# Eighteen expert gate products moved into the recurrence of the second layer, and kept in dead SBUF slots

## The reference

```python
# Mamba block: d_inner = 256, d_state = 16
def step(state, inp):
    dt_t, u_t, b_t, c_t, g_t = inp
    a = a_base[None] * (0.5 + g_t)[..., None]
    decay = jnp.exp(dt_t[..., None] * a)
    state = decay * state + dt_t[..., None] * b_t[:, None, :] * u_t[..., None]
    y_t = jnp.sum(state * c_t[:, None, :], axis=-1) + D_param * u_t
    return (state, y_t)
...
# experts: x is the normalised output of the Mamba block
#   y = sum over e of weight[e] * ((silu(x @ w_gate[e].T) * (x @ w_up[e].T)) @ w_down[e].T)
#   the shared expert (e = 16) has weight 1
```

## Time and profile before

| | |
|---|---|
| three runs | 650.7, 651.13, 652.67 us (median 651.13) |
| the profiled execution's own time | 651.55 us |
| its span, first to last instruction | 649.8 us |
| mean granted TensorE clock | 0.941 of full speed |
| busy: PE, DVE, ACT, POOL | 558.8, 529.8, 361.4, 393.9 us |

### The profile page before, as it was taken

One profiled execution on the slowest core, in us unless ns is written; L12 is line 12 of the kernel. 1 busy time (PEld: TensorE's weight loads), 2 busy tenths in 40 slices (PEclk: granted clock), 3 DMA queues, 4 the chain that ended last, 5 costly groups with the idle time before them and its releaser, 6 DMA issues.

```text
span 649.8 us, 6609 instructions
## 1 busy us (share of the span) xinstructions
PE 558.8 (86%) x1832; PEld 311.2 (48%) x1832; DVE 529.8 (82%) x729; ACT 361.4 (56%) x606; POOL 393.9 (61%) x345
## 2 busy tenths in 40 slices
PE   6698668899999978897868778878979999999997
PEld 3233222376768523333323223223345778888885
DVE  1979997656879678899999999999999857666674
ACT  4675323688123498767746535644455475555553
POOL 0035986752000202399999999999877546666664
PEclk9798977999799998899989868999989999999999
DMA  8000000800120002222223333331214334335330
GB/s 308 15 1 2 0 1 1 344 1 1 66 66 0 2 0 71 75 73 78 73 56 100 95 92 92 115 105 66 96 68 168 96 117 124 127 106 146 112 100 17
DMA packets 23796, 51.59 MB, mean 79 GB/s; under 512 B 2896, under 2 KB 3184, under 8 KB 23248
## 3 DMA queue, kind: packets, MB, share of 16 engines
q1 hardware_dynamic: 23760, 51.17, 24.2%
HBM read 49.83 MB, written 1.33 MB: 79 GB/s over the span
## 4 chain that ended last, share of the span: by engine, by line
PE 36%; DVE 22%; POOL 19%; issue 13%; ACT 9%; DMA 1%; POOLq 0%; DVEq 0%; SPq 0%; ACTq 0%
POOL h_parts L2163 9%; POOL arena L2028 8%; DVE arena L1948 7%; PE ps L1110 7%; PE ps L1045 6%; DVE arena L1923 4%; PE ps L716 3%; DVE arena L1676 3%; PE ps L895 2%; DVE ps L1660 2%; PE ps L912 1%; PE ps L830 1%; PE ps L833 1%; PE ps L831 1%; PE ps L1057 1%
## 5 line engine op out<-in xcount | busy, mean ns | idle before, releaser
L2028 POOL TENSOR_TENSOR arena<-arena 128x512 f32<-128x512 f32 x184 | 225.6, 1249 | 22.6 <-DVE arena L1948 18.5
L1045 PE MATMUL ps<-arena,core 128*128 128x512 f32 x256 | 137.4, 652 | 24.5 <-POOL arena L2028 23.1
L1948 DVE TENSOR_TENSOR_SCAN arena<-ps,carry,arena 128x512 f32<-128x512 f32 x128 | 158.2, 1291 | 0.0
L1505 ACT ACTIVATE ps<-arena,abase 128x512 f32<-128x512 f32 x128 | 88.3, 691 | 93.8 <-DVE arena L1948 92.2
L2163 POOL TENSOR_TENSOR h_parts<-arena,h_parts 128x512 fp32r<-128x512 f32 x68 | 87.7, 1290 | 60.9 <-ACT h_parts L1543 60.0
L1110 PE MATMUL ps<-x_parts,w_hi 128*128 128x512 f32 x272 | 100.7, 409 | 1.0 <-DVE arena L1948 0.5
L1045 PEld LDWEIGHTS ps<-arena,core 128*128 128x128 f32 x256 | 48.3, 201 | 87.2 <-POOL arena L2028 60.8
L1923 DVE TENSOR_TENSOR arena<-ps,arena 128x1024 f32<-128x1024 f32 x64 | 78.4, 1225 | 4.1 <-PE ps L1145 4.0
L2016 DVE TENSOR_TENSOR ps<-ps,arena 128x512 f32<-128x512 f32 x64 | 44.7, 698 | 41.8 <-PE ps L1110 32.9
L1551 ACT ACTIVATE arena<-ps 128x512 f32<-128x512 f32 x68 | 40.5, 597 | 60.5 <-PE ps L1110 60.4
L1110 PEld LDWEIGHTS ps<-x_parts,w_hi 128*128 128x128 f32 x272 | 51.4, 189 | 16.5 <-issue 2.0
(11 more groups left out here) (257 smaller groups left out, 959.3 us busy)
## 6 DMA issues: line engine op xcount, KB each, us to landing
arena<-c_rows SPq DMA_DIRECT2D x64, 256.0 KB, 3.1
arena<-weight_rows SPq DMA_DIRECT2D x64, 256.0 KB, 3.3
arena<-in_wB SPq DMA_DIRECT2D x2, 2048.0 KB, 12.3
arena<-in_wD SPq DMA_DIRECT2D x8, 384.0 KB, 4.1
arena<-in_cstB SPq DMA_DIRECT2D x1, 1368.0 KB, 5.6
wC<-in_wC SPq DMA_DIRECT2D x1, 1056.0 KB, 12.4
x<-in_x SPq DMA_DIRECT2D x4, 256.0 KB, 4.6
arena<-slot_rows SPq DMA_DIRECT2D x4, 256.0 KB, 3.8
```

Of the source, the lines that this page charges most:

```text
L1045: mm(bank(c + 2 * (i % 2)), CORE_("eye"), PRC[:, (2 * q + c) % PR_RING, :], start=False, stop=(n == NS - 1)).then_inc(*done(f"y{n}_{c}", i))
L1505: A(bank(6 + c), ch(DTG[:, c, :], i), ACT.Exp, scale=ABASE[:, c * NS + n:c * NS + n + 1]).then_inc(*done(f"dec{n}_{c}", i))
L1948: nc.vector.tensor_tensor_scan(ST[:, k % ST_RING, :], bank(6 + c), DBU[:, (2 * q + c) % DBU_RING, :], CARRY[:, k:k + 1], ALU.mult, ALU.add ...
L2028: mul = lambda o, a, b: nc.gpsimd.tensor_tensor(o, a, b, ALU.mult)
```

## The change

In words:

- The first 18 gate products (chunk 0 with all 17 experts, and chunk 1 with expert 0) are made by PE during the recurrence, one at the end of each of 18 turns between 31 and 60 (`EARLY_AT`), into PSUM bank 5. ACT copies each to an SBUF slot (`gate_copy`, at the end of the same turn), and the next one waits for that copy. In the expert phase their silu is taken in place from that slot.
- Bank 5 is kept free for them: from turn 30 on `b` has bank 4 alone, so `b(q)` waits for `dbu(q - 1)`, where it waited for `dbu(q - 2)`.
- To find slots, the ring DBU shrinks from 6 to 4 halves. `dbu(q)` thus waits for `st(q - 2)`, where it waited for `st(q - 3)`. The ring ROW shrinks from 8 to 7 rows.
- The down product lies four turns behind (LAG_E = 4), with five slots for its input where there were four.
- At the start of the expert phase `hu0` stands ahead of `y(60)` and `y(61)`, where `hg0` and `hg1` stood around them.

```diff
-LAG_E = 3
-W_SLOTS = 8
+LAG_E = 4
+H_PARTS = LAG_E + 1
+W_SLOTS = 7
...
-C_RING, DBU_RING, PR_RING, ST_RING = 4, 6, 2 * LAG, 8
+C_RING, DBU_RING, PR_RING, ST_RING = 4, 4, 2 * LAG, 8
...
+EARLY_AT = {31: 0, 32: 1, 33: 2, 34: 3, 35: 4, 36: 5, 37: 6, 38: 7, 40: 8, 41: 9, 42: 10, 45: 11, 47: 12, 49: 13, 51: 14, 52: 15, 54: 16, 60: 17}
+EARLY = len(EARLY_AT)
+ONE_BANK = 30
+def b_bank(q):
+    return 4 + q % 2 if q < ONE_BANK else 4
+def b_before(q):
+    return next((p for p in range(q - 1, -1, -1) if b_bank(p) == b_bank(q)), None)
...
             def gate_product(m):
                 i, e = divmod(m, E1 + 1)
                 pe.wait_ge(*upto("x_lo", i))
-                if i == 0:
-                    pe.wait_ge(*upto("w_lo", part_of(3 * e + 2)))
-                if m < 2:
-                    pe.wait_ge(*turn("dbu{}", NQ - 2 + m))
+                if m < EARLY:
+                    pe.wait_ge(*upto("w_lo", part_of(3 * e)))
+                if m < EARLY:
+                    pe.wait_ge(*(expert("hg_copy{}", m - 1) if m else turn("dbu{}", ONE_BANK - 1)))
+                elif m < EARLY + 2:
+                    pe.wait_ge(*(expert("hg_copy{}", EARLY - 1) if m % 2 else turn("dbu{}", NQ - 1)))
                 else:
                     pe.wait_ge(*expert("silu{}", m - 2))
-                product(bank(4 + m % 2), 3 * e, ...
+                product(bank(4 + m % 2 if m >= EARLY else 5), 3 * e, ...
...
                 if q >= 2:
-                    pe.wait_ge(*turn("dbu{}", q - 2))
-                mm(bank(4 + q % 2), sel[:, n, :], ...
+                    pe.wait_ge(*turn("dbu{}", b_before(q)))
+                mm(bank(b_bank(q)), sel[:, n, :], ...
...
                 side_work(q)
+                if q in EARLY_AT:
+                    gate_product(EARLY_AT[q])
             side_work(NQ)
-            gate_product(0)
+            up_product(0)
             y_sum(NQ - LAG)
-            gate_product(1)
             y_sum(NQ - LAG + 1)
-            up_product(0)
...
+            def gate_copy(m):
+                i, e = divmod(m, E1 + 1)
+                act.wait_ge(*upto(f"hg{e}", i))
+                if m in GAM_SLOT:
+                    act.wait_ge(*upto("x_mamba", GAM_SLOT[m]))
+                A(GATED[m], bank(5), ACT.Copy).then_inc(*done(f"hg_copy{e}", i))
             for q in range(NQ):
                 decays(q)
                 side_work(q)
+                if q in EARLY_AT:
+                    gate_copy(EARLY_AT[q])
...
-                act.wait_ge(*upto(f"hg{e}", i))
-                if q >= 2:
-                    act.wait_ge(*expert("hh{}", q - 2))
-                A(SG[:, q % 2, :], bank(4 + q % 2), ACT.Silu).then_inc(*done(f"silu{e}", i))
+                if q < EARLY:
+                    act.wait_ge(*upto(f"hg_copy{e}", i))
+                    A(GATED[q], GATED[q], ACT.Silu).then_inc(*done(f"silu{e}", i))
+                else:
...
```

More of the change, by code:

```diff
@@ L311, in sequences @@
             if 0 < m < TURNS:
-                pe += ([(f"hg{e}", mi)] if m > 1 else []) + [(f"hu{e}", mi)]
+                pe += ([(f"hg{e}", mi)] if m >= EARLY else []) + [(f"hu{e}", mi)]
         if m == 0:
-            pe += [("hg0", 0)] + y_names(q) + [("hg1", 0)] + y_names(q + 1) + [("hu0", 0)]
+            pe += [("hu0", 0)] + y_names(q) + y_names(q + 1)
         elif LAG <= q < NQ + LAG - 1:
@@ L329, in sequences @@
             pool.append(("w_lo", SPLIT_AT[q]))
+        if q in EARLY_AT:
+            j, early = divmod(EARLY_AT[q], E1 + 1)
+            pe.append((f"hg{early}", j))
+            act.append((f"hg_copy{early}", j))
         if 0 <= m < TURNS:
@@ L571, in build @@
         w_parts = [w.rearrange("p (k m) -> p k m", k=WM) for w in (over_arena("w_hi", whi_at, WM * P, f32r), wd_flat)]
[L572 to L576, removed]
+        at = 16400 + 3 * DI * T
+        rings_at = wide_at + 4 * DI * T
+        tail_at = rings_at + (C_RING + 6) * N
+        assert tail_at + N <= WD_AT
+        chunk_of = lambda buf, c, i: buf[:, c, i * N:(i + 1) * N]
+        slot_at = lambda buf, c, i: wide_at + (2 if buf is DTG else 3) * DI * T + c * T + i * N
+        H_HI = [over_arena(f"h_hi{r}", a, N, f32r) for r, a in enumerate([0, N, 2 * N, 3 * N, slot_at(DU, 1, LAST)])]
+        H_LO = [over_arena(f"h_lo{r}", a, N, f32r) for r, a in enumerate([4 * N, 5 * N, 6 * N, 7 * N, slot_at(DTG, 1, LAST)])]
+        SG = [DBU[:, k, :] for k in range(2)]
+        HW = [DBU[:, 2, :], DBU[:, 3, :], chunk_of(DU, 0, LAST)]
+        assert len(H_HI) == len(H_LO) == H_PARTS and len(HW) == H_RING
+        GATED = [chunk_of(DU, 0, 0), chunk_of(DU, 1, 0), chunk_of(DTG, 1, 0), chunk_of(DTG, 0, 0), chunk_of(DU, 0, 1), chunk_of(DU, 1, 1), chunk_of(DTG, 1, 1),
+                 ASIDE[:, 0:N], ASIDE[:, N:2 * N], HD[:, 0:N], area(rings_at + (C_RING + 4) * N, N), area(rings_at + (C_RING + 5) * N, N),
+                 chunk_of(DTG, 0, 1), TF[:, 0:N], chunk_of(DU, 0, 2), chunk_of(DU, 1, 2), chunk_of(DTG, 1, 2), chunk_of(DTG, 0, 2)]
+        assert len(GATED) == EARLY
+        GAM_SLOT = {3: 0, 12: 1, 17: 2}
         wd_part = lambda k: slice(k * WD_STEP, min((k + 1) * WD_STEP, WM))
@@ L1117, in down @@
                 pe.wait_ge(*upto(f"h_hi{e}", i))
-                product(bank(hd_bank(i)), 3 * e + 2, [HWP[:, p, m % 4, :] for p in range(2)], (f"h_lo{e}", i),
+                product(bank(hd_bank(i)), 3 * e + 2, [H_HI[m % H_PARTS], H_LO[m % H_PARTS]], (f"h_lo{e}", i),
                         start=(e == 0), stop=(e == E1)).then_inc(*done(f"hd{e}", i))
@@ L1143, in _ @@
                 if q >= 2:
-                    pe.wait_ge(*turn("dbu{}", q - 2))
-                mm(bank(4 + q % 2), sel[:, n, :], BC[:, i * N:(i + 1) * N], start=True, stop=True).then_inc(*done(f"b{n}", i))
+                    pe.wait_ge(*turn("dbu{}", b_before(q)))
+                mm(bank(b_bank(q)), sel[:, n, :], BC[:, i * N:(i + 1) * N], start=True, stop=True).then_inc(*done(f"b{n}", i))
                 if q >= LAG:
@@ L1547, in _ @@
                 side_work(NQ + q)
-                act.wait_ge(*upto(f"hg{e}", i))
-                if q >= 2:
-                    act.wait_ge(*expert("hh{}", q - 2))
-                A(SG[:, q % 2, :], bank(4 + q % 2), ACT.Silu).then_inc(*done(f"silu{e}", i))
+                if q < EARLY:
+                    act.wait_ge(*upto(f"hg_copy{e}", i))
+                    A(GATED[q], GATED[q], ACT.Silu).then_inc(*done(f"silu{e}", i))
+                else:
+                    act.wait_ge(*upto(f"hg{e}", i))
+                    if q >= EARLY + 2:
+                        act.wait_ge(*expert("hh{}", q - 2))
+                    A(SG[q % 2], bank(4 + q % 2), ACT.Silu).then_inc(*done(f"silu{e}", i))
                 if q:
@@ L1922, in dbu @@
                 a = (DI * q) % DBU_RING
-                tt(DBU[:, a:a + DI, :], bank(4 + q % 2).unsqueeze(1).to_broadcast([P, DI, N]), DU[:, :, i * N:(i + 1) * N],
+                tt(DBU[:, a:a + DI, :], bank(b_bank(q)).unsqueeze(1).to_broadcast([P, DI, N]), DU[:, :, i * N:(i + 1) * N],
                    ALU.mult).then_inc(*done(f"dbu{n}", i))
@@ L2014, in _ @@
                     dve.wait_ge(*expert("h_lo{}", q - H_RING))
[L2015 to L2016 removed]
+                tt(bank(6 + k) if e < E1 else HW[q % H_RING], bank(6 + k), GATED[q] if q < EARLY else SG[k], ALU.mult).then_inc(*done(f"hh{e}", i))
                 if e < E1:
@@ L2020, in _ @@
                     dve.wait_ge(row_loaded[r % W_SLOTS], 16 * (r // W_SLOTS + 1))
-                    tt(HW[:, h, :], bank(6 + k), ROW[r % W_SLOTS], ALU.mult).then_inc(*done(f"hw{e}", i))
+                    tt(HW[q % H_RING], bank(6 + k), ROW[r % W_SLOTS], ALU.mult).then_inc(*done(f"hw{e}", i))
                 if i and e == LAG_E + 1:
```

34 lines of the change are left out of this document (21 added, 13 removed).

## The result

The changed kernel takes 662.27 us (median of 4 runs, 661.1 to 665.97), beside 651.13 us of the kernel before (650.7 to 652.67). A fourth run of the kernel before took 955.08 us, is counted as slow and left out; nothing measured here says why. The ratio is 1.0169, 95% interval 1.0143 to 1.0195: 11.0 us of 651. It is beyond the forecast of 653.0 and outside its range. The profiled execution took 661.1 us with a span of 659.3 us; before it was 651.55 and 649.8. The traces are compared by their spans, +9.5 us.

A forecast was written before the change was run, and what follows sets the result against it. It took DVE to bound the recurrence and PE the experts. Recurrence +7.2 - 1.85 + 1 = +6.35 us and experts -4.5 us sum to +1.85 us, a median of 653.0 us, range 647.5 to 658.

The forecast's parts named there:

- part 1: Recurrence, DVE: the DBU ring of 4 makes dbu wait for the scan just ahead; 0.13 us in 55 turns, +7.2 us.
- the rival that it is free: Recurrence, DVE: dbu's wait on its own engine costs nothing, giving 648.6 us; chance 0.12.
- part 2: Recurrence: two old waits of dbu for PE, 1.42 and 0.43 us, are absorbed; -1.85 us.
- Parts 2 and 3: Recurrence: old dbu waits absorbed, -1.85 us; new waits from the gate products in PE's turns, +1 us (0 to 5).
- the rival of a late PE: Recurrence, turns 31 to 54: PE becomes late at half clock, 5 us of waits instead of 1, giving 657.0; chance 0.2.
- hh14 is at 527.5 ... hh18 at 534.8: Experts, behind rsF: predicted start times of these steps, hh18 coming 4.5 us earlier than before.
- part 4: Experts: eighteen gate products gone, partly offset by y(60), y(61), half clock and DVE's pace; -4.5 us.
- the walk: Experts from hu0 on: steps followed with their old durations and the program's waits, hh1 at 499.8 to hh18 at 534.8.
- LAG_E costs 0: Experts: the down product lying four turns behind changes nothing, as the end hangs on the last h_lo; 0 us.
- That PE stays the bound and wins 11.2 us: Rival, experts: DVE's side work and rsF hide behind PE, giving 646.3 us; chance 0.13.
- The rival that the change gains nothing in the first 18 turns: Experts: DVE and its loop hold these turns at their old length, gain 0, giving 657.5 us; chance 0.1.

The follow-up runs named there:

- b_wait_st0: Kernel before, DBU ring still 6, dbu(q) waiting for st(q - 2) of half 0, the scan last but one: 651.78 us, ratio 1.0003.
- b_wait_st1: Kernel before, DBU ring still 6, dbu(q) waiting for st(q - 2) of half 1, the scan just ahead: 661.32 us, ratio 1.0163.
- b_onebank: Kernel before with b in bank 4 alone from turn 30 on, nothing else changed: 651.88 us, ratio 1.0004.
- a_ring6: Changed kernel with the DBU ring back at 6 halves, so 16 early gate products instead of 18: 652.33 us, ratio 1.0001.
- a_order: Changed kernel with y(60) and y(61) back ahead of hu0: 657.85 us, ratio 1.0096.
- a_fill16: Changed kernel with 11 matmuls, result unread, added on PE at expert turn 16: 660.34 us, ratio 1.0137.
- a_split: Changed kernel, ring of 4, with dbu cut into two halves, each waiting for a scan one instruction further back: 654.98 us, ratio 1.0061.
- a_lag3: Changed kernel with the down product three turns behind instead of four (LAG_E = 3): 662.43 us, ratio 1.0182.
- b_ring4: Kernel before with the DBU ring at 4 halves and nothing else changed: 662.66 us, ratio 1.0158.

## Why the prediction was wrong

**Step that failed first: the size of part 1.** The mechanism was the one foretold. The own wait ends the overlap and adds a signal, once in each undisturbed turn, and the rival that it is free fell: `b_wait_st0` and `b_wait_st1` differ by one instruction in what they wait for, and by 10.4 us. The Trainium skill, "VectorE: DVE Perf Modes", section "The DRAIN you can't avoid", on which that rival leaned, does not hold for this pair of instructions: a wait on another VectorE operation is free here only where that is not the one just ahead. The copies that the page timed are in no run here. The term was mis-sized. I had taken 0.13 us a turn from `hh` and `hw` and from the mixes and taps of the earlier trace rows, all of them TENSOR_TENSOR or SCALAR_TENSOR_TENSOR. Behind a scan it is 0.20 to the `dbu` (0.10 of overlap, 0.10 and not 0.03 of gap), and from `dbu` to the scans 1.14 instead of 1.11, which has no cause in these runs, less 0.02 in the scans themselves: together 3.69 - 3.48 = 0.21 us. Over the same 55 turns that is 11.6 and not 7.2 us, beyond my upper bound of 8.7: none of its rows had a scan as the one waited for. The ring alone measured +9.9, which is this term less what part 2 absorbs.

**Parts 2 and 3 held.** The waits of 1.42 and 0.43 us are gone. New waits come to 1.06 us, 1 was forecast, and `dbu` waits 2.8 us for PE, about 3 was forecast. The recurrence is 11.6 - 1.85 + 1.06 = 10.8 by these terms, 10.6 by the trace. `x_lo` was indeed what the first product waited for:

```profile
379.27 0.51 PE L1142 MATMUL ps<-x_parts,w_hi 128*128 128x512 f32 x1 [2.13 <-POOL x_parts L2173]
```

but PE was not late for `dbu` there. That `b` has one bank costs nothing (`b_onebank`), and with the products in its turns as well it is 0.7 us (`a_ring6`), so the rival of a late PE fell too.

**Step that failed second: "hh14 is at 527.5 ... hh18 at 534.8", in part 4.** Up to `hh14` the walk was 1.1 us off in 33: a half clock after 493 and 3.4 us for `y(60)` and `y(61)` were foreseen, and `a_order` showed them, 3.4 us shorter up to `hh14`. At `rsF` I wrote that PE "runs dry" and then priced everything behind it at full clock. It ran dry, and the granted clock fell to 0.50 behind it: 10.21 us instead of 7.3, 2.9 us of the 4.0 by which the experts' 4.5 us shrank to 0.5. The walk itself was right at full clock: `a_fill16` and `a_split`, whose clock stayed at 1.00, both took 7.36 us. And `a_split` had the hole too, so that the clock falls was likely after such a hole and not certain (three of the four traces with some 2.6 us), which makes this term depend on luck. I had used the same reasoning at `hu0`, and had not asked the question again at the next hole that the change makes.

**The rest.** LAG_E costs 0, as forecast (`a_lag3`). That PE stays the bound and wins 11.2 us fell: only between `hh4` and `hh13` was it nearly so (busy 16.32 of 17.26 us). The rival that the change gains nothing in the first 18 turns gave the right number, 0.5 us, for another reason: those turns did become shorter by 5.4 us, and lost it at both ends.

**How the errors add.** 4.4 us in part 1 and 4.0 in part 4, less the 0.6 that the rest gave, are 7.8; the profiled execution missed its forecast of 653.4 by 661.1 - 653.4 = 7.7. The median lies 1.2 us above that execution, where 0.4 below was assumed, which is the rest of the 9.3 us between 653.0 and 662.27. The two terms did not cancel because one was half again as large and the other nearly vanished.

**What stays open.** Why the signal of a scan comes 0.07 us later than that of a TENSOR_TENSOR, what holds the `dbu` at 454.03 for 0.46 us (not the moved products: `b_ring4` has the same wait at the same turn), when a hole of 2.6 us brings the clock down, and how much of the 2.85 us that `a_fill16` gains in its trace reaches the total (2.1 by the ratios); no run was made for these.

## What to carry to other kernels

A ring that is shortened until an instruction waits for the one just ahead of it on its own engine cost VectorE its overlap on every turn here; keep one instruction between the two, or cut the waiting one so that each half looks one further back. Price such a wait by a neighbour of the same kind as the one waited for. When work is taken out of a matmul engine that was packed, look at every place where it now runs dry, not only the first, and ask what clock it comes back with. Filling the hole took 2.1 and 2.5 us off here, at the edge of what the runs can tell; the products saved had taken off nothing by themselves (`a_ring6`).

## What the runs showed of the hardware beyond that

- A TENSOR_TENSOR that waits for a scan of 128x512 just ahead starts 0.10 us behind its end; one that waits for a TENSOR_TENSOR of that size, 0.03 us; one that waits for neither starts 0.10 us ahead of a scan's end. A wait on the instruction last but one costs nothing (651.78 beside 651.62 us).
- Nearly the same idle time of PE did not always bring the clock down. Beside `a_split` and its 2.63 us, this holds for shorter holes. In two of the kernels it stood idle at `rsF` for 1.94 and 1.96 us between full stretches. With the ring of 6 alone:

```profile
530.05 0.50 PE L1142 MATMUL ps<-x_parts,w_hi 128*128 128x512 f32 x1 [1.94 <-DVE arena L2071]
...
532.05 1.74 PE L1114 MATMUL ps<-wC,arena 128*128 128x16 f32 x8
```

and with the ring of 6 and the new order:

```profile
531.27 0.51 PE L1142 MATMUL ps<-x_parts,w_hi 128*128 128x512 f32 x1 [1.96 <-DVE arena L2071]
...
533.11 1.06 PE L1114 MATMUL ps<-wC,arena 128*128 128x16 f32 x8 [0.18 <-ACT arena L1515]
```

The first fell to half clock behind it (10.75 us from `hh14` to `hh18`), the second did not (8.06 us). What decided is open; each is one profiled execution.
